# Gates, q, k and v as three float16 passes from unit 4 on, a fourth buffer of exponentials, and a new plan

## What is computed

```python
# 1 gated recurrence (w.r.t. n = layernorm(x))
i, f, o = sigmoid(n @ Wi + bi), sigmoid(n @ Wf + bf), sigmoid(n @ Wo + bo)
s = tanh(n @ Ws + bs)
h = f_t * h + i_t * s_t                      # a scan over the 4096 tokens
x = x + layernorm(n + o * h) * gamma + beta
# 2 and 4 feed-forward with token shift, the same weights twice
x = x + sigmoid(xr @ W_r.T) * (relu(xk @ W_k.T)**2 @ W_v.T)   # xr, xk: mixes of n with the token before
# 3 causal attention, 16 heads of 16
q, k, v = n @ Wq.T + bq, n @ Wk.T + bk, n @ Wv.T + bv
x = x + softmax(mask(q @ k.T / 4)) @ v @ Wo.T + bo
```

## Time and profile before

| | |
|---|---|
| median of 3 runs | 1749.54 us (1749.43 to 1753.24) |
| span of the profiled execution | 1749.5 us |
| TensorE busy | 1709.4 us, 98% |
| VectorE busy | 1509.9 us, 86% |
| ScalarE busy | 1342.8 us, 77% |
| GpSimd busy | 688.8 us, 39% |
| TensorE's granted clock | 1.00 throughout (2.4 GHz) |
| instructions | 45658 |

### The profile page before, as it was taken

One profiled execution on the slowest core, in us unless ns is written; L12 is line 12 of the kernel. 1 busy time (PEld: TensorE's weight loads), 2 busy tenths in 40 slices (PEclk: granted clock), 3 DMA queues, 4 the chain that ended last, 5 costly groups with the idle time before them and its releaser, 6 DMA issues.

```text
span 1749.5 us, 45658 instructions
## 1 busy us (share of the span) xinstructions
PE 1709.4 (98%) x18242; PEld 641.3 (37%) x18242; DVE 1509.9 (86%) x2975; ACT 1342.8 (77%) x2781; POOL 688.8 (39%) x994
## 2 busy tenths in 40 slices
PE   8999999999999999999999999999999999999997
PEld 6554444344433333334333333332332322222324
DVE  6778979986899999998998999999999999999802
ACT  3336677767677878876888879889889899898894
POOL 3348666478562453428336225220311220212201
PEclk9999999999999999999999999999999999999999
DMA  4132021003002000020000020000002000000000
GB/s 113 56 74 57 27 46 31 18 21 62 28 18 48 13 30 13 8 48 25 6 24 8 21 29 6 24 13 2 7 14 34 18 4 3 14 1 14 2 7 13
DMA packets 57000, 43.71 MB, mean 25 GB/s; under 512 B 8788, under 2 KB 56788, under 8 KB 56788
## 3 DMA queue, kind: packets, MB, share of 16 engines
q1 hardware_dynamic: 54548, 39.75, 9.4%
q10 hardware_dynamic: 2240, 1.05, 0.5%
HBM read 24.00 MB, written 16.25 MB: 23 GB/s over the span
## 4 chain that ended last, share of the span: by engine, by line
PE 60%; DVE 13%; ACT 4%; issue 2%; POOL 2%; SPq 0%; DMA 0%; ACTq 0%; POOLq 0%; DVEq 0%
PE psum L1804 21%; PE psum L1783 12%; PE psum L1751 12%; DVE span_max L1539 12%; PE psum L1608 7%; PE psum L1600 6%; ACT probs L1283 2%; ACT probs L1294 1%; PE psum L1593 1%; PE psum L1813 1%; PE psum L1758 1%; DVE rows L1478 0%; DVE shift_parts L1554 0%; POOL rows L1100 0%; DVE small L1388 0%
## 5 line engine op out<-in xcount | busy, mean ns | idle before, releaser
L1539 DVE TENSOR_REDUCE span_max<-psum 128x1 f32<-128x512 f32 (+3 forms) x2304 | 1313.7, 636 | 98.6 <-PE psum L1751 73.8
L1283 ACT ACTIVATE probs<-psum 128x512 f32<-128x512 f32 (+3 forms) x2148 | 1040.7, 570 | 173.3 <-PE psum L1783 170.1
L1804 PE MATMUL psum<-probs,v_aug 128*17 128x512 f32 (+3 forms) x4608 | 564.9, 562 | 1.3 <-ACT oT L1303 0.8
L1751 PE MATMUL psum<-k_stack,q_stack 48*128 48x512 f16 (+3 forms) x2304 | 533.2, 363 | 4.4 <-DVE span_max L1539 2.7
L1783 PE MATMUL psum<-q_stack,k_stack 50*128 50x512 f16 (+3 forms) x2304 | 521.0, 364 | 5.5 <-DVE span_max L1539 0.7
L1783 PEld LDWEIGHTS psum<-q_stack,k_stack 50*128 50x128 f16 x2304 | 148.7, 93 | 388.7 <-ACT probs L1283 272.4
L1751 PEld LDWEIGHTS psum<-k_stack,q_stack 48*128 48x128 f16 x2304 | 156.0, 93 | 287.9 <-DVE span_max L1539 214.3
L1149 POOL TENSOR_SCALAR_AFFINE_SELECT probs<-probs 128x512 f32<-128x512 f32 x128 | 81.1, 637 | 254.3 <-ACT probs L1283 209.7
L1804 PEld LDWEIGHTS psum<-probs,v_aug 128*17 128x17 f32 x4608 | 77.7, 95 | 136.4 <-issue 114.7
L1188 ACT ACTIVATE rows<-psum,cols 128x256 f32<-128x256 f32 x128 | 53.9, 479 | 56.0 <-PE psum L1600 52.6
L1758 PE MATMUL psum<-mask_keys,mask_rows 64*128 64x64 bf16 x1024 | 93.5, 189 | 0.0
(11 more groups left out here) (139 smaller groups left out, 1548.1 us busy)
## 6 DMA issues: line engine op xcount, KB each, us to landing
q_stack<-q_parts SPq DMA_DIRECT2D x192, 32.0 KB, 2.0
k_stack<-k_parts SPq DMA_DIRECT2D x42, 128.0 KB, 5.0
rows<-in_x SPq DMA_DIRECT2D x16, 256.0 KB, 2.7
q_parts<-rows SPq DMA_DIRECT2D x32, 128.0 KB, 2.0
k_parts<-rows SPq DMA_DIRECT2D x32, 128.0 KB, 2.0
out<-rows SPq DMA_DIRECT2D x16, 256.0 KB, 2.2
x_rows<-rows SPq DMA_DIRECT2D x14, 256.0 KB, 2.2
rows<-x_rows SPq DMA_DIRECT2D x14, 256.0 KB, 2.7
```

Source lines behind the costliest of these rows:

```text
L1283: act.activation(probs[:, tile % PROBS, i, q0:], bank(b)[:, q0:], ACT.Exp, scale=SCALE / QK_SCALE).then_inc(exp_done, 1)
L1539: nc.vector.tensor_reduce(span_max[:, s % SPAN_RING, row:row + 1, k0 // SPAN:k0 // SPAN + 1], bank(b)[:, 0:k1 - k0], AX.X, ALU.max).then_i ...
L1751: ins = nc.tensor.matmul(bank(b)[:, 0:k1 - k0], q_stack[row:row + SCORE_ROWS, s % Q_RING, u, qt * P:(qt + 1) * P], k_stack[row:row + SCORE ...
L1804: ins = nc.tensor.matmul(pv_bank[32 * h:32 * h + VW, q0:], v_aug[:, j, g * HG + h, :], probs[:, tile % PROBS, h, q0:], start=(j == 0), sto ...
```

## The change

1. **Products in parts.** For units 4 to 15 (`SPLIT_FROM`) the copy of `x1T` and `x3T` writes a float16 high part (scaled by 2^10), and a new VectorE operation (`x1T.lo`, `x3T.lo`) writes the float16 remainder from PSUM. The seven weights of the gates, q, k and v have the same two parts. A half is now 2 channel blocks x 3 passes (high x high, low x high, high x low) x 4 strips = 24 float16 matmuls. They wait for the remainder, and the transposes' bank is held until it is taken. The scale is taken back by ScalarE, as a factor of the activation that reads the product.
2. **Preparing them.** After the second norm of unit 2: ScalarE squares five weights (`g.square`), TensorE sums them over channels (`gbound`, 3 jobs), VectorE and GpSimd turn the sums into powers of two (`g.max`, `g.clip`, `g.pow`, `g.scale`, `qk.scale`), ScalarE writes the seven high parts (`w.hi`) and VectorE the low ones (`w.lo`). The float32 weights are loaded into the second half of `v_aug`, unused until unit 8; its ones are set later (`ones.late`), behind unit 3's products and all `w.lo`, and v's copy of unit 8 waits for that.
3. **Fourth buffer.** Once the gates of unit 15 are issued, their weights' place is the fourth buffer for exponentials (`probs_of`, `PROBS_LATE`), and scores may run four tiles ahead.
4. **Plan.** A half in parts is planned at 650 instead of 865 ns, `WORTH` has one value for each of 32 steps, with other numbers throughout, and pairs of exponentials are taken together from step 28 instead of 30. The order of all engines is another.

```diff
+SPLIT_FROM = 4
+X_UNIT = 2.0 ** 10
+PARTED = ("f", "i", "o", "s", "av", "aq", "ak")
+PROBS_LATE = 4
-STAGE = (0, 0, 0, 1, 1, 2, 2, 3)
-        W = {n: w[STAGE[STEPS[TILES[min(scored, len(TILES) - 1)][0]][1]]] for n, w in WORTH.items()}
+        W = {n: w[TILES[min(scored, len(TILES) - 1)][0]] for n, w in WORTH.items()}
+PRODUCT = 650
-EXPS_SINCE = 30
+EXPS_SINCE = 28
...
+        ring = PROBS_LATE if gates_done() else PROBS
-        if scored < len(TILES) and ("place", TILES[scored][0]) in seen and scored < summed + PROBS:
+        if scored < len(TILES) and ("place", TILES[scored][0]) in seen and scored < summed + ring:
...
+                    if u >= SPLIT_FROM:
+                        act.activation(x1T_parts[:, 0], bank_chan(BANK["x1T", u]), ACT.Copy,
+                                       scale=X_UNIT).then_inc(x1T_ready, 1)
...
+                elif op[0] in ("x1T.lo", "x3T.lo"):
+                    dve.wait_ge(hi_ready, u + 1)
+                    nc.vector.scalar_tensor_tensor(out=parts[:, 1], in0=bank_chan(BANK[n, u]), scalar=X_UNIT,
+                                                   in1=parts[:, 0], op0=ALU.mult, op1=ALU.subtract)\
+                        .then_inc(lo_ready, 1)
+                elif op[0] == "w.lo":
+                    nc.vector.scalar_tensor_tensor(out=w_parts[n][:, 1], in0=raw[n],
+                                                   scalar=w_scale[:, op[1]:op[1] + 1], in1=w_parts[n][:, 0],
+                                                   op0=ALU.mult, op1=ALU.subtract).then_inc(w_lo, 1)
...
+            TERMS = ((0, 0), (1, 0), (0, 1))
+
+            def channels_in_parts(b, w, src, e):
+                for k in range(CT):
+                    for n, (x, y) in enumerate(TERMS):
+                        for c in range(0, P, COLUMNS):
+                            ins = nc.tensor.matmul(bank_chan(b)[c:c + COLUMNS, e],
+                                                   w[:, y, k, e * P + c:e * P + c + COLUMNS], src[:, x, k],
+                                                   start=(k == 0 and n == 0),
+                                                   stop=(k == CT - 1 and n == len(TERMS) - 1))
...
+                        if u >= SPLIT_FROM:
+                            pe.wait_ge(x1T_lo, u - SPLIT_FROM + 1)
+                        else:
+                            pe.wait_ge(x1T_ready, u + 1)
```

More of the change, by code:

```diff
@@ L154, with cost_of, job_read @@
           "aT", "x3": "proj", "x3.copy": "proj", "shift.copy": "shift", "norm": "out", "scale.bound": "bound",
-          "bo.add": "bo"}
+          "bo.add": "bo", "g.max": "gbound", "x1T.lo": "x1T", "x3T.lo": "x3T"}
+def cost_of(k):
+    if k[0] in ("f", "i", "s", "o", "q", "kk", "v") and k[1] >= SPLIT_FROM:
+        return PRODUCT
+    return COST["PE"][k[0]]
+def job_read(k):
+    if k[0] in ("x1T.copy", "x3T.copy") and k[1] >= SPLIT_FROM:
+        return None
+    return (READER[k[0]],) + k[1:] if k[0] in READER else None
 def followed():
@@ L197, in followed @@
     op(("scale.apply",), ("scale.raise",), normalized(0, LN_F1))
+    for i in range(len(BOUND_PAIRS)):
+        op(("g.square", i), normalized(2, LN_F1))
+        op(("gbound", i), ("g.square", i), ("prepare",))
+        op(("g.max", i), ("gbound", i))
+    op(("g.clip",), *[("g.max", i) for i in range(len(BOUND_PAIRS))])
+    op(("g.pow",), ("g.clip",))
+    op(("g.scale",), ("g.pow",))
+    op(("qk.scale",), ("scale.apply",))
+    for i, n in enumerate(PARTED):
+        op(("w.hi", i), ("qk.scale",) if n in ("aq", "ak") else ("g.scale",))
+        op(("w.lo", i), ("w.hi", i))
+    op(("ones.late",), *[(n, SPLIT_FROM - 1, 1) for n in ("f", "i", "s", "o", "q", "kk", "v")],
+       *[("w.lo", i) for i in range(len(PARTED))])
     op(("bo",), ("bound",))
@@ L247, in followed @@
                 op((parts, u), (n + ".part1", u))
-        op(("v", u, 0), ("x3T.copy", u))
+        op(("v", u, 0), x3T_ready, *([("w.lo", PARTED.index("av"))] if u == SPLIT_FROM else []))
         op(("v", u, 1), ("v", u, 0))
-        op(("v.copy", u), ("v", u, 1))
+        op(("v.copy", u), ("v", u, 1), *([("ones.late",)] if u == LATE_KEYS // UT else []))
         if u % 2:
@@ L587, in schedule @@
             division = DIVISION.get(k[0], "full")
-            free["PE"] = at + PACE * COST["PE"][k[0]]
+            free["PE"] = at + PACE * cost_of(k)
             half_free = [free["PE"]] * 2
@@ L617, in schedule @@
             division = "half"
+            if widened is None and gates_done() and pair == 0 and len(score_left) == 2:
+                widened = scored
+                order.append(("widen", scored))
             half_free[how] = at + 4 + PACE * width(scored) / 2.4
@@ L1611, in tokens_out, with tokens_in_parts @@
                 return ins
+            TERMS = ((0, 0), (1, 0), (0, 1))
[7 more added lines that the diff above has]
+                                                   stop=(k == CT - 1 and n == len(TERMS) - 1))
+                return ins
+            def tokens_in_parts(b, w, src, j):
+                for k in range(CT):
+                    for n, (x, y) in enumerate(TERMS):
+                        for c in range(0, P, COLUMNS):
+                            ins = nc.tensor.matmul(bank_tok(b)[c:c + COLUMNS, j],
+                                                   src[:, x, k, j * P + c:j * P + c + COLUMNS], w[:, y, k],
+                                                   start=(k == 0 and n == 0),
+                                                   stop=(k == CT - 1 and n == len(TERMS) - 1))
+                return ins
             maxed = scores = 0
@@ L1727, in _ @@
                     ins.then_inc(full["bound"], 1)
+                elif name == "gbound":
+                    _, i, b = op
+                    claim(b, sums_read, GMAX[i])
+                    pe.wait_ge(filled, FILLS)
+                    pe.wait_ge(squared, GSQUARE[i])
+                    for w, n in enumerate(BOUND_PAIRS[i]):
+                        for k in range(CT):
+                            ins = nc.tensor.matmul(bank_tok(b)[:, w], ones, weights[n][:, k],
+                                                   start=(k == 0), stop=(k == CT - 1))
+                    ins.then_inc(full["gbound"], 1)
                 elif name == "bo":
```

311 lines of the change are left out of this document (247 added, 64 removed), and 9 rows, old and new, of the table WORTH.

## The result

The changed kernel takes **1733.8 us** (median of 4 runs, 1733.5 to 1734.7), the kernel before, beside it, 1750.7. The ratio is 0.9903 (95% interval 0.989 to 0.9917): 16.8 us faster, half of the 33.5 forecast, within the range. The profiled execution's span is 1732.9 us. The medians of before lay between 1750.3 and 1752.5, and a difference is good to some 2.5 us, so that effects under 3 us are hints only. Two runs with a lower granted clock stand apart: one of the four of e19 (2637.7 us, clock 0.56) is left out, and one of the kernel before beside e19 and e20 (1767.4 us, clock 0.965) widens the intervals of these two.

A forecast was written before the change was run, and what follows sets the result against it. The prediction took TensorE to set the pace, with VectorE nearly level after 1094 us. Its terms summed as 1749.5 - 31.7 + 2 + 4 - 8 = 1715.8, so 1716 us, range 1692 to 1738.

The forecast's parts named there:

- (a): TensorE's products: 168 halves fall from 0.865 to 0.648 us each, 36.4 us less streaming.
- That rival (1805): TensorE's products: weight loads aren't hidden, a half takes 1.2 us and the kernel 1805 us; chance 0.05.
- (b): Whole kernel: 87% of the products' 36.4 us arrives at the end, -31.7 us (bounds -25 and -36.4).
- (c): VectorE: 24 remainders of 0.68 us, 16.4 us of work, delay the products behind them by +2 us overall.
- (d): Start of the kernel: preparing the weights' parts (squares, sums, maxima, high and low parts) costs +4 us (0 to +10).
- (e): Fourth buffer and new plan: 40 pairs of visits of the weighted sum merge, -8 us (-32 to +15).
- halves 0.65 apart: Sign on TensorE: float16 product halves follow each other at 0.65 us, 24 matmuls each.
- Last gate near 925: Sign on TensorE: the last gate product comes near 925 us rather than 954.
- last v near 1288: Sign on TensorE: the last v product comes near 1288 us.
- From the last v to the end: Sign at the kernel's end: this time, 431 us before, shrinks by under 10 us.
- the new order eats the gain: Rival, whole kernel: banks come free late, some 1,700 changes cost 0.02 us more each, +34, 1750 us; chance 0.07.
- VectorE takes over: Rival, 219 to 1094 us: VectorE's added work cancels part of the gain, giving 1736 us; chance 0.13.

The follow-up runs named there:

- e19: Kernel before with VectorE's maxima and GpSimd's in-place elementwise steps over half of their columns: 1721.7 us, ratio 0.9817.
- e20: Kernel before with maxima and GpSimd's in-place steps halved, and products from unit 4 on cut to 0.648 us a half: 1696.4 us, ratio 0.9673.
- e12: Kernel before, its order kept, with products of gates, q, k and v from unit 4 on cut to 0.648 us a half: 1743.5 us, ratio 0.995.
- e11: Changed kernel, its order kept, with a fourth pass (low x low), so products are as long as in float32: 1760.6 us, ratio 1.0047.
- e16: Kernel before with each of VectorE's maxima over half of its columns: 1727.0 us, ratio 0.9859.
- e22: Kernel before with GpSimd's in-place steps halved, maxima whole, and products from unit 4 on cut to 0.648 us a half: 1725.5 us, ratio 0.986.
- e2: Changed kernel with the weights' scales set to constants, so no squares, sums, maxima or power: 1727.9 us, ratio 0.9866.
- e6: Changed kernel with GpSimd's norm of unit 5 of the first layer moved behind unit 3's reciprocal root: 1729.3 us, ratio 0.9871.
- e1: Changed kernel, its order kept, without the third pass of the products in parts: 1725.1 us, ratio 0.9852.
- e14: Changed kernel with GpSimd's norm of unit 5 moved later and the squares of the weights kept as bfloat16: 1727.7 us, ratio 0.9861.
- e10: Changed kernel with 27 more warming transposes filling a 3.26 us stall of TensorE near the start: 1734.8 us, ratio 0.9903.

## Where the prediction was right and where it failed

(a) **The product: right.** 36.4 us less of streaming were forecast, 36.5 counted; 0.648 us for a half, 0.65 read. The Trainium skill ("TensorE: Matmul & The Clock Gate", Part 3, "The mechanism") lets a load hide only behind matmuls of another row group; 24 matmuls of all 128 rows, each with its own load, within 0.65 us disagree, as the earlier trace rows did. That rival (1805) is out.

(b) **The share that arrives: this step failed.** 87% was taken because the chain of waits held VectorE and ScalarE for only 13.4%. In the old order 9 of 36 us arrive (e12), which is 22.7 less than the 31.7 forecast; in the new one 25 (e11 to the change), 6.9 less. Those 25 are counted with an order tuned for short products, in which long ones are at a loss, and are the kinder measure. The chain's shares describe the execution as it ran. They do not say who is just behind, and with all lists fixed to lengths of 0.865 several engines are. Behind TensorE came GpSimd, at 39% busy absent from the sum, then the maxima (e16 to e22). The chain could have hinted at it: followed back, that of the kernel before ends at 317.5 us, so that the earlier trace rows say nothing of the time from 94.8 to there, where a third of the saved halves lies, and in 219 to 575 its lines of GpSimd, each of 1.0% or less, come to 7.7%. A remade order recovers a part.

(c) **Remainders: about right.** +2 forecast, 2.4 measured with an interval that includes none. VectorE stands at 93.9% in 219 to 1094 as forecast, and TensorE's matmuls idled 0.5 us in all for a remainder (its weight loads 2.1), under the 3 that the forecast named.

(d) **Preparation: mis-sized.** +4 forecast (bounds 0 and 10); squares, sums and their followers cost 6 (e2) and the new order's late norm 5 (e6), 11 together if they add up. That unit 4's parts might stall the start was named. What did was a GpSimd step that waited for a store, the kind of step that the forecast's own list of moves leaves out.

(e) **Plan and fourth buffer: mechanism wrong, size open.** Long products in the new order cost +8.0 (e11). Taking from that 6.2, 4.8 and 2.4 for the parts above leaves -5.4 for buffer and plan, where -8 was forecast; this is a remainder, not a measurement, and it hangs on the path. Starting from the old order instead, the cut is worth 9.0 (e12), and -21.2 is left for buffer and plan. No visits merged. By the records only 11 of the 576 tiles have their scores four tiles ahead of the sum, which three buffers do not allow.

Against the forecast of -33.7 and with the measured -16.8, 6.9 of the missing 16.9 us are (b), 7.0 (d), 0.4 (c), 2.6 (e) by the first path. By the second (b) misses 22.7 and (e) gives 13.2 more than forecast. Either sum closes because (e) is what is left over, so that closing proves nothing. What holds on both paths: (b) took too much and (d) cost 7 more than forecast. That the time fell into the range is in part luck: (b) had bounds of -25 and -36.4, and the two measures of it, -9.0 and -24.8, lie outside.

The signs that the prediction named: halves 0.65 apart, right. Last gate near 925: wrong, the new order puts it at 1088 (954 before); last v near 1288, it came at 1279:

```profile
L1846 PE MATMUL psum<-rows,w_gates x2304: 270/273/421, 104.3 to 1088.2; 128*32 128x256 f16 x192
```

```profile
L1856 PE MATMUL psum<-w_av,rows x576: 272/273/283, 201.3 to 1279.4; 128*32 128x256 f16 x192
```

From the last v to the end are 453 us, 22 more than before, not fewer. Such marks move with the order and tell little of the gain.

The rival "the new order eats the gain" had some truth with another mechanism: banks came free late in the first 219 us, and changes cost no more each (the gap at a change is 0.098 us in the median of both kernels). "VectorE takes over" was half true: behind GpSimd, in the old order. In the new order GpSimd's steps were not halved; what stops three quarters of e1's cut there is open beyond the longer waits for maxima. What holds the last 10 us of the cut with both halved is open. ScalarE's exponentials are the longest share besides TensorE in the chain there (6.3% of 219 to 575 in e20), which is a hint and no proof. Whether a new search of worths for e14's start gives more wasn't tried.

## What to carry to other kernels

In a hand-fixed order a cut on the bottleneck is not worth its share of the chain of waits: here a quarter arrived in the order of before, and two thirds when measured in the one made for the new length. Try the cut alone on the chip in the old order (skip part of the work) before pricing the rest, and look for the runner-up with pairs of runs, long and short, that free one other engine each; an engine that is 40% busy can be it. Look at the granted clock of every run that is compared. Follow every moved step to the transfer it waits for, and to the other transfers that are under way then.

## What the hardware showed that I had not expected

A store of 256 KB landed after 6.4 us in the change and after 5.0 in the kernel before, against a median of 2.3 and 2.1 in 219 to 600 us. Both slow ones were issued behind six transfers of 128 KB on ScalarE's queue, of which six and five were still in flight and the last landed at 108.1 and 96.4, close to the stores (107.7 and 96.7). That they share the bandwidth is likely, but no run moved them apart. The wait was there before too, and cost GpSimd 2.2 us instead of 4.4.

TensorE's granted clock went to its half level (1.2 GHz) for 6.8 us after 3.26 us of idling (product halves took 1.47 us in place of 0.84 for 24 records), and giving it back (e10) gained nothing, since that time was waiting anyway. It also fell without such a stall: in e12, at 186.0 and 640.0 us, the longest idle gaps of the matmuls in the 8 us before were 1.0 and 0.6 us.
